# Two attention phases of a routed-expert network: steps written out, work moved between ACT, DVE and Pool, and scatters a step later

## The reference

```python
x = x + tanh(g_xattn[0]) * L0_xattn(layernorm(x), ctx, ctx)
x = x + tanh(g_ffn[0])   * L0_ffn(layernorm(x))
x = x + tanh(g_xattn[1]) * L1_xattn(layernorm(x), ctx, ctx)
x = x + tanh(g_ffn[1])   * L1_ffn(layernorm(x))
# xattn, 16 heads of 16: q from x, k and v from ctx (layer 0: v = ctx @ Wv.T + bv)
scores = einsum('bhsd,bhtd->bhst', q, k) / 4
#   layer 0: scores = where(triu(ones, 0) with [0, 0] off, -inf, scores)
#   layer 1: scores = where(arange(S) < valid_len[b], scores, -1e6)
out = softmax(scores) @ v @ Wo.T          # layer 0: + bo
# ffn: 8 experts, the top 2 of each token
#   layer 0: softmax(x @ gate.T), silu experts of 256 hidden, plus a shared silu expert
#   layer 1: cosine of x @ Wp.T with sim_matrix rows, gelu experts of 1024 hidden
```

## Time and profile before

| | |
|---|---|
| median of 3 runs | 1856.92 us |
| lowest and highest | 1847.23 and 1857.61 us |
| the profiled execution | 1850.12 us |
| its span | 1848.4 us |
| mean granted clock of TensorE in it | 0.936 |
| layer zero's attention phase, by the timeline | about 0 to 574 us |
| experts of layer zero | about 590 to 815 us |
| layer one's attention phase | about 820 to 1384 us |
| experts of layer one | about 1398 us to the end |

### The profile page before, as it was taken

How to read it: one execution, slowest core, us unless ns; L and a number is a source line. 1 busy time by engine, 2 the same in 40 slices (tenths; PEclk the granted TensorE clock), 3 DMA queues, 4 the chain that set the end, 5 groups by cost and what they waited for, 6 DMA issues and landing times. The chain is left out here.

```text
span 1848.4 us, 44757 instructions
## 1 busy us (share of the span) xinstructions
PE 1509.7 (82%) x14491; PEld 1253.5 (68%) x14492; DVE 1165.4 (63%) x3254; ACT 707.4 (38%) x1516; POOL 724.4 (39%) x616
## 2 busy tenths in 40 slices
PE   3799988999982777844888888888752999999997
PEld 2677877788761566633566666666432999999996
DVE  4678876878762334334778888887752455555543
ACT  2344534444430111102354544554421444444443
POOL 4234333344233655553123333333235344446422
PEclk9899999999996999975799999999985999999998
DMA  2433333232214666651323332332225233333322
GB/s 89 106 83 102 95 86 97 81 105 79 80 36 137 115 120 112 115 104 54 99 78 109 92 111 81 110 83 82 71 69 177 59 69 91 91 89 85 87 46 40
DMA packets 211174, 167.03 MB, mean 90 GB/s; under 512 B 23042, under 2 KB 203620, under 8 KB 210788
## 3 DMA queue, kind: packets, MB, share of 16 engines
q1 hardware_dynamic: 179556, 124.56, 24.4%
q0 software_dynamic: 28416, 40.03, 11.7%
q10 hardware_dynamic: 3072, 0.79, 0.2%
HBM read 63.40 MB, written 50.51 MB: 62 GB/s over the span
## 5 line engine op out<-in xcount | busy, mean ns | idle before, releaser
L839 DVE TENSOR_REDUCE a_row_max<-a_scores 128x2 f32<-128x512 f32 x256 | 172.3, 683 | 53.3 <-PE a_scores L1455 49.7
L1693 POOL DMA_INDIRECT out_rows<-e_y,e_token x68 | 110.5, 1625 | 239.2 <-DVE e_y L1749 219.3
L1163 ACT ACTIVATE a_probs<-a_scores_t 128x384 f32<-128x384 f32 (+1 forms) x256 | 132.2, 546 | 163.6 <-PE a_scores_t L1470 82.1
L1163 ACT ACTIVATE a_w_rows<-a_scores_t 128x384 f32<-128x384 f32 (+1 forms) x256 | 138.7, 543 | 142.6 <-PE a_scores_t L1473 74.2
L1775 ACT ACTIVATE e_h<-e_h,t_up_bias 128x256 f32<-128x256 f32 x272 | 110.3, 444 | 206.2 <-PE e_h L1811 206.2
L685 POOL DMA_INDIRECT routed_rows_dram<-r_rows,r_slot x128 | 125.6, 981 | 96.4 <-issue 96.4
L1826 PE MATMUL e_y_bank<-e_down_hi,e_hidden_hi 128*128 128x256 f32 x544 | 157.9, 290 | 0.4 <-DVE e_hidden_lo L1722 0.3
L1811 PE MATMUL e_h<-e_xs_hi,e_up_hi 128*128 128x256 f32 x544 | 155.4, 286 | 1.8 <-DVE e_xs_lo L1714 1.6
L1811 PE MATMUL e_h<-e_xs_lo,e_up_hi 128*128 128x256 f32 x544 | 154.7, 284 | 0.0
L1811 PE MATMUL e_h<-e_xs_hi,e_up_lo 128*128 128x256 f32 x544 | 154.6, 284 | 0.0
L1826 PE MATMUL e_y_bank<-e_down_lo,e_hidden_hi 128*128 128x256 f32 x544 | 153.8, 283 | 0.0
(11 more groups left out here) (267 smaller groups left out, 4673.5 us busy)
## 6 DMA issues: line engine op xcount, KB each, us to landing
a_q_stack<-a_parts SPq DMA_DIRECT2D x384, 64.0 KB, 2.7
a_k_stack<-a_parts SPq DMA_DIRECT2D x384, 64.0 KB, 2.6
e_xs_rows<-routed_rows_dram SPq DMA_DIRECT2D x76, 258.0 KB, 3.2
a_ctx_rows<-in_ctx SPq DMA_DIRECT2D x32, 256.0 KB, 3.1
t_up<-in_L_ffn_W SPq DMA_DIRECT2D x8, 1024.0 KB, 5.0
t_down<-in_L_ffn_W SPq DMA_DIRECT2D x8, 1024.0 KB, 7.6
x_rows<-in_x SPq DMA_DIRECT2D x16, 256.0 KB, 3.1
x_mid_dram<-x_rows SPq DMA_DIRECT2D x16, 256.0 KB, 2.9
```

The source lines that it names most:

```text
L839: nc.vector.reduce_max(row_max[:, :, h], bank[:].rearrange("p (c t) -> p c t", c=TC), AX_X).then_inc(maxed, 1)
L1163: nc.scalar.activation(probs[h % NP][:, 0:width], scores_t[h % 2][:, 0:width], ACT.Exp).then_inc(probs_ready, 1)
L1693: pool.indirect_dma_start(out=x_acc, out_offset=bass.IndirectOffsetOnAxis(ap=token[p][:, c:c + 1], axis=0), in_=y[p][:, c, :], in_offset=N ...
```

## The change

1. HEAD = B + 5 and TAIL = 0: all 21 steps are written out; no loop is left in the phases.
2. `evac_k` of layer zero and `evac_v` of both layers go from DVE to ACT. Layer zero's bias bv isn't added to v any more: a softmax sums to one, so bv can go through Wo once, in the preamble, and be added to bo (`bv_spread` on DVE, a turn on PE, `bv_cols` on ACT, `bv_mixed` on PE, an addition and the gate on DVE). Pool's bias of x waits for it.
3. The negative maxima are cut in two bf16 parts (MP = 2): two DVE operations for each half instead of four, and one DMA issue on ACT for both rows instead of three. `split_max(i, 1)` comes ahead of `add_shared`.
4. Layer one's `valid` and `mask_row` are made by Pool (`mark_valid`, last in its step, for batch i+3); SP waits for them before it sends the mask rows.
5. The slots of layer one move: gate 1 to 2, projection of the heads 4 to 5, v 6 to 8, ranks 9 to 10, context 12 to 13, and their followers with them. Layer zero keeps its slots.
6. `send_rows` works on batch i-3 instead of i-2 and stands behind `rest`, ahead of `invert_norm` and the third part. `copy_rows` on ACT goes to slot 10, for batch i-2. Pool runs two steps more.

The core of the diff:

```diff
     lo, hi = first + head, last + 1 - tail
...
+    if lo < hi:
+        with eng.Fori(lo // 2, hi // 2) as pair:
...
-        FIRST, LAST, HEAD, TAIL = -3, B + 1, 7, 8
+        GATE_AT, O_AT, V_AT, RANK_AT, CTX_AT = (1, 4, 6, 9, 12) if soft else (2, 5, 8, 10, 13)
+        FIRST, LAST, HEAD, TAIL = -3, B + 1, B + 5, 0
...
+            def mark_valid(i):
+                b, p = i.at(3), i.par(3)
+                n = slice(b, b + 1)
+                need(pool, k_ready, b)
+                nc.gpsimd.tensor_scalar(valid[:], iota_t[:], lens_f[:, n], None, ALU.is_lt).then_inc(valid_done, 1)
+                need(pool, stacked[1][p], i.half(3) * 16 * STACK_DMAS)
+                nc.gpsimd.tensor_scalar(mask_row[p][:], iota_t[:], lens_f[:, n], neg_col[:, 0:1], ALU.is_ge, ALU.mult).then_inc(valid_done, 1)
...
             def send_rows(i):
-                b, p = i.at(-2), i.par(-2)
-                wait_apart(pool, rows_ready, b + 1, consts_ready, 1)
-                pool.wait_ge(rows_copied, b + 1)
+                b, p = i.at(-3), i.par(-3)
...
                     nc.gpsimd.tensor_tensor(rest[:], qk[:], parts[p][:, :, 0, :], ALU.subtract).then_inc(part_rest, 1)
+                if i.has(-3):
+                    send_rows(i)
                 if not soft and i.has(-2):
                     invert_norm(i)
...
-                if i.has(-2):
-                    send_rows(i)
-
-            pipeline(pool, step, B, FIRST, LAST, HEAD, TAIL)
+                if not causal and i.has(3):
+                    mark_valid(i)
+
+            pipeline(pool, step, B, FIRST, LAST + 2, HEAD + 2, TAIL)
...
-                nc.vector.scalar_tensor_tensor(out=max_rest[:, :, hs], in0=row_max[:, :, hs], scalar=-1.0, in1=max_parts[:, :, half, 0, :],
-                                               op0=ALU.mult, op1=ALU.subtract).then_inc(max_r1, 1)
-                dve.wait_ge(max_r1, n)
-                nc.vector.tensor_copy(max_parts[:, :, half, 1, :], max_rest[:, :, hs]).then_inc(max_mid, 1)
-                dve.wait_ge(max_mid, n)
-                nc.vector.tensor_tensor(max_parts[:, :, half, 2, :], max_rest[:, :, hs], max_parts[:, :, half, 1, :],
-                                        ALU.subtract).then_inc(max_ready, 1)
+                nc.vector.scalar_tensor_tensor(out=max_parts[:, :, half, 1, :], in0=row_max[:, :, hs], scalar=-1.0,
+                                               in1=max_parts[:, :, half, 0, :], op0=ALU.mult, op1=ALU.subtract).then_inc(max_ready, 1)
...
+            def evac_k(i):
+                b = i.at(2)
+                act.wait_ge(k_done, b + 1)
+                nc.scalar.activation(qk[:, KC:2 * KC, :].rearrange("p c s -> p (c s)"), stage[0][:], ACT.Copy).then_inc(k_ready, 1)
+
+            def evac_v(i):
+                b, p = i.at(1), i.par(1)
+                act.wait_ge(v_done, b + 1)
+                need(act, pv_done, (b - 1) * GROUPS)
+                nc.scalar.activation(v_pad[p][:, PAD:].rearrange("p (n w) -> p n w", w=VW)[:, :, 0:HD],
+                                     stage[1][:].rearrange("p (n w) -> p n w", w=HD), ACT.Copy).then_inc(v_ready, 1)
...
-                for j in range(3):
-                    act.dma_start(q_stack[p][MAX_ROW + j:MAX_ROW + j + 1, half * HH:half * HH + HH, :],
-                                  turned[j * HH:(j + 1) * HH, :]).then_inc(max_stacked[half][p], 16)
+                act.dma_start(q_stack[p][MAX_ROW:MAX_ROW + MP, half * HH:half * HH + HH, :], turned[:]).then_inc(max_stacked[half][p], 16)
```

More of the change, by code:

```diff
@@ L57, in pipeline @@
     assert lo % 2 == 0 and (hi - lo) % 2 == 0
[L58 to L61, removed]
+    if lo < hi:
+        with eng.Fori(lo // 2, hi // 2) as pair:
+            with eng.If(pair * 2 < while_below) if while_below is not None else nullcontext():
+                step(Step(pair, 0, count))
+                step(Step(pair, 1, count))
     for i in range(hi, last + 1):
@@ L495, in layer_phase @@
         acc_tiles = x_acc[0:tokens, :].rearrange("(b c p) d -> b p c d", c=TC, p=P)
[L496 removed]
+        N_CONSTS = 2 if causal else 1
         N_READY = 8
@@ L985, in step @@
                     divide(i, -1, 1)
-                if i.has(2):
+                if not causal and i.has(2):
                     evac_k(i)
@@ L1211, in step @@
                     stack_max(i, 0, 1)
+                if causal and i.has(2):
+                    evac_k(i)
                 for h in range(H):
@@ L1214, in step @@
                         exponentials(i, h)
+                    if h == V_AT + 1 and i.has(1):
+                        evac_v(i)
                     if h == 1 and i.has(2):
                         cut_hi(i)
-                    if h == 1 and i.has(-2):
+                    if h == GATE_AT and i.has(-2):
                         evac_gate(i)
@@ L1222, in step @@
                         cut_mid(i)
-                    if h == 6 and i.has(-2):
+                    if h == GATE_AT + 5 and i.has(-2):
                         route_exps(i)
@@ L1226, in step @@
                         evac_xn(i)
-                    if h == 12 and i.has(3):
+                    if h == CTX_AT and i.has(3):
                         evac_ctx(i)
@@ L1230, in step @@
                         stack_max(i, 1, 0)
-                    if h == 13 and i.has(-1):
+                    if h == 10 and i.has(-2):
                         copy_rows(i)
@@ L1257, in _ @@
             pe.wait_ge(consts_ready, N_READY)
+            if causal:
+                pe.wait_ge(bv_spread, 1)
+                for m in range(KC):
+                    last = nc.tensor.transpose(stage[0][:, m * P:(m + 1) * P], bv_rows[:, m].rearrange("p n half d -> p (n half d)"), keep.ident[:])
+                last.then_inc(bv_turned, 1)
+                pe.wait_ge(bv_copied, 1)
             pe.wait_ge(r_loaded, 16 * N_LOADS)
@@ L1267, in _ @@
                 pe.wait_ge(prep_copied, 3)
+                for m in range(KC):
+                    last = nc.tensor.matmul(stage[1][:, D:2 * D], bv_cols[:, m, :], wo_t[:, m, :], start=(m == 0), stop=(m == KC - 1))
+                last.then_inc(bv_mixed, 1)
+                pe.wait_ge(bo_gated, 1)
             else:
```

123 lines of the change are left out of this document (64 added, 59 removed).

## The result

The changed kernel takes 1884.39 us in the median (1882.6 to 1888.08, 4 runs) against 1857.14 before (4 runs): a ratio of 1.0172, interval 1.0149 to 1.0195. It is slower by 1.7%, where 1822 and a gain were forecast. In the profiled executions the span grows from 1848.4 to 1880.9.

What follows compares the result with a forecast made beforehand. PE was taken to bound layer zero, a ring of waits layer one. Terms −12.7 − 20.4 + 1.4 + 9 − 8 = −30.7 gave 1819.4 from the profiled 1850.1, adjusted towards the median to 1822; range 1784 to 1843.

Steps and rivals of the forecast that it cites:

- scale_scores at M + 12.85: Layer one: from M, when split_max(1) is ready, four scatters ahead of invert_norm put scale_scores 12.85 us later.
- the way back: Layer one, scale_scores to the next split_max(1) being ready: 21.1 us falls to 17.2, then 17.9 with late scores and Pool's masks.
- the base: Layer-one step without anything new: DVE loses 2.26 us of work, two PE waits shrink, 29.99 falls to 27.4.
- −8 for steps 1, 2, 14 and 15: Layer-one steps without the scatter stall take the gain of 2 us each; bounds −4 to −10.
- +9 − 8 = +1: Layer one in all: scatters add 0.8 us in each of 11 full steps, +9; the four other steps gain 8.
- Rival D: Layer one, head 7 of steps 3 to 13: PE runs dry, then a lower clock, 6.3 us a step, 1882; chance 0.07.
- Layer zero: Its steps gain 33.1 us: 12.7 from writing out the loop, 20.4 from relieving DVE, 1.45 a full step.
- The long steps: Layer zero's two loop-return steps, 35.68 and 37.11 us, fall to about 30.0 when written out: 12.7 us gone.
- The bias through Wo: Layer zero's preamble: two small DVE operations and handshakes ahead of the first turn of xn, +1.4 us, bounds 0 and +3.
- Slots: Layer one's later slots for gate, update, v, rank and context move waits within the ring, leaving its length: 0.
- Rival C: Layer one: Pool's masks slow DVE's heads 12 to 14 by up to 1.4 us a step, +14, 1836; chance 0.10.
- Rival B: Written-out code stalls elsewhere on instruction fetch, so the loop's 12.7 us gain is lost: 1835; chance 0.11.

Runs made afterwards that it cites:

- e1: Changed kernel with Pool's four scatters moved behind invert_norm and the third part; ratio 0.9777 to the kernel before, layer-one step 31.4 us.
- g2: Changed kernel with layer one's scale_scores and followers three head slots later and invert_norm ahead of the scatters; ratio 0.9987 to the kernel before.
- g3: Changed kernel with layer one's scale_scores and followers three slots later and scatters in two pairs, behind rest and the third part; 1829.69 us against 1852.23 before.
- b3: Kernel before with only ACT's evictions, the bias through Wo and the two-part maxima; ratio 0.9851 to the kernel before.
- f1: Changed kernel with the loop of three pairs back in layer zero alone; 1887.3 us against 1884.8 for the changed kernel, ratio 1.0208 to the kernel before.
- b2: Kernel before with only the four scatters moved as the change moves them; ratio 1.0102 to the kernel before, layer-one step 37.6 us.
- f2: Changed kernel with layer one's slots as before the change; ratio 0.9860 to the kernel before, layer-one step 36.2 us.
- f3: Changed kernel with layer one's scale_scores and followers three slots later and the masks made by DVE again; ratio 0.9773 to the kernel before.
- b0: Kernel before, unchanged, run again on a chip of the second kind; steps of 36.0 us in layer zero and 32.4 in layer one.
- a0: Changed kernel, unaltered, run again on a chip of the second kind; ratio 0.9921 to the kernel before, layer-one step 35.8 us.
- e3: Changed kernel with the scatters back at the end of Pool's step, for batch i-2; ratio 1.0029 to the kernel before, layer-one step 33.5 us.
- e2: Changed kernel with only invert_norm taken ahead of the four scatters, the third part still behind them; ratio 0.9851 to the kernel before.

## Why the prediction was wrong

**Right: what Pool does to scale_scores.** "scale_scores at M + 12.85": M is 1167.05, scale_scores starts at 1179.83, M + 12.8. The wait, said to be 3 to 5 us, is 5.1.

**Wrong: the way back.** The step that failed is the one that counts "From scale_scores at 1198.26 to the next M": 17.9 was worked out by taking operations out of DVE's queue, and 22.7 was measured (1179.83 to 1202.54). Three things were missing. DVE isn't what sets this half: once PE has stood, it has the work of nine heads, v, the turns of xn, context and routing rows, and q ahead of the next M. That takes 19.2 us from 1183.35 on, PE is busy for 16.9 of them, and DVE waits for it. The work runs in part at 1.2 GHz (a mean clock of 0.91). And scale_scores falls beside Pool's third part and lasts 2.21 instead of 0.48, +1.7; before, it lay where Pool had no large operation. How the 4.8 us divide among the three isn't shown. In e1, at full clock and with scale_scores at 0.48, the way back is 23.1 and PE is busy for 20.1 of it, so the first alone is enough to miss 17.9; e1's half holds a stop as well.

The Trainium skill ("GPSIMD Engine Reference", "Specifications") names contention between Pool and VectorE for VectorE instructions in a 2-port mode or with two SBUF inputs. The trace shows contention here: scale_scores ends 0.23 us behind Pool's third part both in the changed kernel and in g2, and takes 0.48 where Pool is idle. It has one tensor input and two scalars, and which of the page's two conditions it meets no run shows. The prediction used the rule against the masks and not against the operation that the move pushed beside L725.

**Wrong: the base.** "without anything new the step would be 29.99 − 2.6 = 27.4". With the wait cured, a step lasts 31.1 (e1), 30.6 (g3), never 28. Of the waits of the earlier trace rows the one on evac_k went and the one on r_xn_t shrank from 1.4 to 0.8, but 0.9 for ACT's copy of the turned maxima came new and the one for row maxima grew from 0.9 to 1.7 (g3). The relief of DVE bought little in layer one: 0.7 a step in b3, and nothing is seen of it in g3. DVE and ACT spend much of the step waiting for PE, and PE for them; that this is the reason is argued, not shown. Of the −8 for steps 1, 2, 14 and 15 nothing came either: up to step 3 layer one took 1.0 us more than before. Its forecast was +9 − 8 = +1 in all, and +59.5 was measured up to step 13.

**Rival D, given 0.07, was the outcome.** Its place (head 7, the eighth score of the step, is the one at 1183.35), its mechanism (PE runs dry, then the lower clock) and its price, 6.3 us a step, against 35.9 − 30.0 = 5.9 measured (PE stands 3.4 longer and works 2.5 longer, where 3.0 and 3.3 were priced), and its 1882 against 1884, all held. What spoke against it, "PE has 4 us of slack work in a step of layer one", confused idle time with cover: the idle time was in pieces elsewhere in the step, and a wait of 4 us in one place added to it.

**Layer zero, right in sum and partly for the wrong reason.** −33.1 was forecast for its steps, −31.0 measured (−25.0 and −6.0, the second with the experts in it). The level steps last 29.1 and not 28.5, since one wait for a row maximum stays:

```profile
PE a_scores L1481 <- DVE a_row_max L850: 0.6, 1, 0.6
```

Here PE gained 0.8 a step, not 1.45. The long steps are gone, as said, but f1 shows that writing out isn't what it takes: with ACT evicting k and DVE's code shorter, the loop costs 2.5 us. That the return alone can hold DVE up is shown by b2 (3.18 us with the scatters far off). The Trainium skill ("Runtime: NRT & Kernel Launch", "Instruction fetch mechanics") says that a taken branch out of the window must be fetched; b2 agrees, f1's return doesn't show it, nor did layer one's. Why f1 has none no run shows.

**Small terms.** The bias through Wo was to cost 1.4 and cost 2.2 up to the first step. Slots: 0 forecast; they gain 0.3 a step and lose some 7 us at the start of layer one, 0.6% of the time on balance (f2). Rival C, masks that slow DVE: not borne out with the scatters behind `rest`, where masks on Pool gain 1.0 a step (f3). Rival B, stops elsewhere in straight code: not on the first kind of chip; on the second the stops are there but follow the scatters, not the code. Nothing of this kind was in the range, because nothing in the one trace showed it.

## What to carry to other kernels

Before work is put ahead of a small operation on a side engine, ask who waits in order for that operation; five us of DMA issue on Pool became 4 us of idle TensorE and 2 us of slower clock in each step. When a stall is moved into a ring, the way back is not the sum of one engine's queue but the longest over the engines, each with the work that piled up behind the stall. Idle time in pieces is no cover for a stall in one piece, and relief on an engine that waits for others is worth little: 0.7 us a step in b3, where 2 to 2.6 were expected.

## What the runs showed of the hardware

Four of five chips showed the stop behind the scatters, about 6 us a step at its worst place, and one didn't, with the same kernel: 1937 to 1941 us against 1852. The sign of the whole change hangs on it: 1.0172 and 1.0186 on the first kind, 0.9921 on the second. There the move of the scatters costs 5.2 us a step in layer one and saves 4.0 in layer zero when it is made alone (b2 against b0), and costs 2.3 and saves 4.7 within the changed kernel (a0 against e3): alone it is a loss (1.0102), and with the rest of the change a gain (0.9921, against 1.0029 and 1.0012 without it). A DVE operation of 0.48 us took 2.21 beside a 128x1024 subtraction on Pool, and 1.49 in g2. An idle PE of 3.8 to 4.1 us was followed by a lower clock, 0.61 us for two matmuls that take 0.38 at the full one; one of 2.2 us (e2) as well, its steps having a mean clock of 0.95. An idle stretch that long isn't needed for it: g2's steps of 33 us have 0.95 too, with no wait of PE above 0.9.
